# Cross-attention and feed-forward block on one core: two layer-norm scalings to ScalarE, residual add and shifts to GpSimd, bias by matmul

## The chip, the cores and the metric

One core of a Trainium2 chip. The metric is the device time of one execution in microseconds (us); lower is better.

## The reference, cut to what matters

```python
x = x + xattn0(layernorm(x), ctx, ctx)   # 16 batches x 8 heads; a head takes 16 rows of 256
x = x + ffn0(layernorm(x))               # 16 experts, one shared weight
x = x + xattn1(layernorm(x), ctx, mask)
x = x + ffn1(layernorm(x))               # half of the tokens, w1, gelu, w2

def layernorm(x): return (x - mean(x)) / sqrt(var(x) + 1e-5)

# xattn0: qk = qh . kh * scale; ret = softmax(qk) . vh      (x, ctx: [16, 128, 256])
# ffn0:   logits = xf @ router_w + router_b; S = softmax(logits); G, idx = top_k(S.T, 128)
#         out = xf[idx] @ expert_w + expert_b; y[idx] += G * out
```

## The kernel before, in words

The program runs in three stages. The first (to about 250 us) is the first attention with the expert product behind it; the second (to about 295 us) finds each expert's threshold digit by digit; the third is the second attention and the last feed-forward. The change touches the first stage; in the third it only puts buffers elsewhere.

The first stage handles two batches in a unit, eight units (`NU`), of 16 steps j: a step is one head of one batch. Every engine has its own list of instructions written by hand, `unit(...)` of each block, and `if j == ...` places extra work behind a step. Units 2 and 3 are one loop of the program, the others are written out. i is 0 for the unit's first batch and 1 for its second; the second is finished in the next unit.

- **TensorE** computes in step j the scores of a head that lies 8 steps ahead (`scores`, L1094), for the row maxima, and the transposed scores of the head 2 steps ahead (`scores_t`, L1107), for exp. Each has two banks, so scores wait until VectorE has reduced the bank, and transposed scores until ScalarE has taken theirs. Behind every fourth step comes the product with the values (`values`, L1121). `xn_t` transposes the normalised rows (L1144), `yw` multiplies them with the expert and router weights (L1150), `ctx_t` (L1137) and `max_t` (L1130) are transposes too.
- **VectorE** reduces row maxima (L531), makes the low part of the negated maxima (`neg_low`, L536), and finishes a batch: `gather_parts` (L542, L544) sorts numerators and denominators of even and odd heads, `invert` (L549), `bring_over` (L553, L556), `add_x1` (residual add L563, statistics L565 and L567), `scale_rows` (layer norm, L573), `take_yw` (L580, L581, both with a bias). For a later unit it computes the statistics of x (`stats_q`, L479 to L482) and the scaled queries (`scale_q`, L487).
- **ScalarE** does the exps (L895), `take_even` (L936, L937), `neg_high` (L901), the two DMA issues of `send_neg_max` (L906), `take_xnt` (L943), and the roundings of k and q to bf16: `high_k` (L918), `mid_k` (L922), `high_q` (L926), `mid_q` (L930).
- **GpSimd** does the remainders of these roundings (`rest_k` L336, `low_k` L341, `rest_q` L345, `low_q` L350), the inverse roots (L355, L357), `keep_rows` (L366) and `fill_values` (L374).
- **SyncE** writes the three parts of k and q to DRAM, stages the next unit's x and context (`load_stage`) and loads the stacks from DRAM.

Queries and keys are prepared three units ahead: unit u makes those of unit u + 3. All staging for unit u + 4 waits until q of unit u + 3 is split (`q_split`), since `ctx_stage` and `x_stage` exist once:

```python
sp.wait_ge(s["q_split"], u)                       # load_stage
dve.wait_ge(s["staged"], 32 * (u + 1))            # stats_q
```

## Time and profile before

| | us |
|---|---|
| median of 3 executions | 420.0 |
| lowest, highest | 419.33, 426.34 |
| the profiled execution, its own time | 422.43 |
| its span in the trace | 420.2 |
| VectorE busy | 317.7 (76%) |
| TensorE matmuls busy | 279.6 (67%) |
| ScalarE busy | 167.6 (40%) |
| GpSimd busy | 94.8 (23%) |

The span runs from the first to the last instruction; 2.2 us of the execution's own time lie outside it. PE is TensorE's matmuls, DVE VectorE, ACT ScalarE, POOL GpSimd, SPq and ACTq the instructions by which SyncE and ScalarE issue DMAs. In a row, `out<-in` are tiles by the program's names (digits are left out of some), then shapes and count. Instructions that follow one another closely overlap by up to 0.1 us in the trace, so a duration is a little more than the distance between two starts.

### The profile page before, as it was taken

To read this page: it belongs to the slowest core of one execution; us is meant where nothing else is said; L and a number is where in the kernel's file an instruction comes from. 1 tells how busy PE (TensorE), PEld (TensorE's weight loads), DVE (VectorE), ACT (ScalarE), POOL (GpSimd) and SP (SyncE) were. 2 spreads that over 40 slices of the span, in tenths; PEclk is the share of its full clock that TensorE was granted. 3 is DMA by queue.
4 is the path that set the end of the run, shared out by engine and by line. 5 is a ranking of instruction groups with operands and counts; after the bars stand their busy time and mean duration, and the time that the engine had idled before them with its cause. 6 is when DMAs were issued, how large, how long until landed. Compare 5 with 4: busy or idle time off the path is not lost.

```text
span 420.2 us, 7370 instructions
## 1 busy us (share of the span) xinstructions
PE 279.6 (67%) x1872; PEld 182.5 (43%) x1872; DVE 317.7 (76%) x989; ACT 167.6 (40%) x397; POOL 94.8 (23%) x222
## 2 busy tenths in 40 slices
PE   1134777777886877877778621001559999999996
PEld 0011333353442544444334310000438988888884
DVE  5847458899989889799986748888377888787631
ACT  4110543464654536464556500000111566445631
POOL 1101323352415224111111110000133322333200
PEclk9999975789698886899989965555555999999999
DMA  2789388959294581740000380000000000000001
GB/s 88 202 189 153 98 221 187 166 150 165 71 197 79 145 126 54 146 80 1 2 1 2 100 301 0 1 0 2 1 0 0 2 25 25 25 0 25 26 27 51
DMA packets 24379, 32.90 MB, mean 78 GB/s; under 512 B 4066, under 2 KB 22434, under 8 KB 22818
## 3 DMA queue, kind: packets, MB, share of 16 engines
q1 hardware_dynamic: 23842, 32.48, 33.5%
q10 hardware_dynamic: 512, 0.13, 0.2%
q8 instruction: 10, 0.16, 0.2%
q14 instruction: 15, 0.12, 0.1%
HBM read 24.02 MB, written 8.39 MB: 77 GB/s over the span
## 4 chain that ended last, share of the span: by engine, by line
DVE 35%; PE 33%; issue 12%; DMA 8%; ACT 4%; POOL 3%; SPq 2%; DVEq 1%; ACTq 1%; POOLq 0%
DVE row_max L531 7%; PE t_bank L1355 5%; PE pv_bank L1273 5%; PE pv_bank L1121 4%; DMA q_stack<-q_parts_dram 4%; DVE denom_inv L549 3%; PE score_bank L1094 3%; PE scoret_bank L1107 3%; PE t_bank L1150 2%; PE score_bank L1336 2%; DMA q_parts_dram<-q_parts 2%; ACT probs L895 2%; DMA q_stack<-neg_max 2%; PE score_bank L1303 2%; DVE junk L705 1%
## 5 line engine op out<-in xcount | busy, mean ns | idle before, releaser
L895 ACT ACTIVATE probs<-scoret_bank 128x512 f32<-128x512 f32 x128 | 73.1, 596 | 52.5 <-PE scoret_bank L1107 42.3
L531 DVE TENSOR_REDUCE row_max<-score_bank 128x2 f32<-128x512 f32 x112 | 74.4, 679 | 24.3 <-PE score_bank L1094 23.1
L1107 PE MATMUL scoret_bank<-q_stack,k_stack 98*128 98x256 bf16 (+1 forms) x256 | 54.6, 301 | 28.1 <-ACT probs L895 18.7
L1094 PE MATMUL score_bank<-k_stack,q_stack 96*128 96x256 bf16 (+1 forms) x240 | 53.6, 314 | 19.1 <-DMA q_stack<-q_parts_dram 11.0
L355 POOL TENSOR_SCALAR var_eps<-mv 128x1 f32<-128x1 f32 x48 | 9.2, 192 | 189.5 <-DVE mv L567 106.9
L1107 PEld LDWEIGHTS scoret_bank<-q_stack,k_stack 98*128 98x128 bf16 (+1 forms) x256 | 24.2, 104 | 46.6 <-ACT probs L895 20.5
L1121 PE MATMUL pv_bank<-probs,values_ones 128*32 128x256 f32 x512 | 42.0, 455 | 1.0 <-ACT probs L895 1.0
L1094 PEld LDWEIGHTS score_bank<-k_stack,q_stack 96*128 96x128 bf16 (+1 forms) x240 | 21.7, 105 | 47.8 <-issue 15.3
L1273 PE MATMUL pv_bank<-q_stack,k_stack 128*128 (+1 forms) x256 | 36.0, 285 | 0.4 <-ACT q_stack L1070 0.4
L1045 ACT COPY xnt<-score_bank 128x256 f32<-128x256 f32 x16 | 6.0, 373 | 74.6 <-PE score_bank L1294 74.6
L1273 PEld LDWEIGHTS pv_bank<-q_stack,k_stack 128*128 128x128 f32 x256 | 33.9, 202 | 1.3 <-issue 0.9
L1355 PE MATMUL t_bank<-k_stack,probs 128*128 128x256 f32 x128 | 29.4, 382 | 0.0
L357 POOL TENSOR_TENSOR rstd<-var_eps,minus_half 128x1 f32<-128x1 f32 x48 | 26.1, 543 | 8.8 <-POOL var_eps L355 8.8
L549 DVE RECIPROCAL denom_inv<-denom 128x256 f32<-128x256 f32 x16 | 27.7, 1732 | 0.0
L1355 PEld LDWEIGHTS t_bank<-k_stack,probs 128*128 128x128 f32 x128 | 23.7, 190 | 2.9
L1254 PE MATMUL t_bank<-count,same_expert 128*128 128x3 bf16 x15 | 2.8, 187 | 31.4 <-DVE equal L705 31.4
L1150 PE MATMUL t_bank<-wr_moving,xnt 128*128 128x272 f32 x64 | 22.0, 474 | 1.2 <-ACT xnt L943 1.2
L1064 ACT ACTIVATE probs<-pv_bank,b1s 128x128 f32<-128x128 f32 x64 | 17.6, 379 | 11.8 <-PE pv_bank L1273 11.7
L1121 PEld LDWEIGHTS pv_bank<-probs,values_ones 128*32 128x32 f32 x512 | 15.0, 122 | 16.2 <-issue 9.0
L1144 PE MATMUL t_bank<-ident,xn 128*128 128x128 f32 x32 | 7.0, 303 | 18.5 <-DVE xn L573 10.2
L1137 PE MATMUL t_bank<-ident,ctx_stage 128*128 128x128 f32 x32 | 7.6, 383 | 16.3 <-DMA x_stage<-in_x_dram 16.3
L1150 PEld LDWEIGHTS t_bank<-wr_moving,xnt 128*128 128x128 f32 x64 | 13.4, 234 | 8.1 <-issue 4.1
(182 smaller groups left out, 534.5 us busy)
## 6 DMA issues: line engine op xcount, KB each, us to landing
q_stack<-q_parts_dram SPq DMA_DIRECT2D x48, 128.0 KB, 6.9
k_parts_dram<-k_parts SPq DMA_DIRECT2D x24, 128.0 KB
q_parts_dram<-q_parts SPq DMA_DIRECT2D x24, 128.0 KB
k_stack<-k_parts_dram SPq DMA_DIRECT2D x8, 384.0 KB, 4.6
ctx_stage<-in_ctx_dram SPq DMA_DIRECT2D x8, 256.0 KB, 3.2
x_stage<-in_x_dram SPq DMA_DIRECT2D x8, 256.0 KB, 3.9
k_stack<-k_parts_dram SPq DMA_DIRECT2D x8, 256.0 KB, 5.3
xs<-in_x_dram SPq DMA_DIRECT2D x8, 256.0 KB, 7.3
```

The lines of the kernel that those rows point to most:

```text
L355: pool.tensor_scalar(work, variance, EPS, factor, ALU.add, ALU.mult).then_inc(s[summed], 1)
L357: pool.tensor_tensor(dst, work, minus_half[:, 0:dst.shape[1]], ALU.pow).then_inc(s[ready], 1)
L531: dve.tensor_reduce(row_max[:, i, :, h], score_bank[bank_of][:, :].rearrange("p (m n) -> p m n", m=2), AX.X, ALU.max).then_inc(s["max_done ...
L549: dve.reciprocal(denom_inv[:, i, :], denom[:, i, :]).then_inc(s["div_step"], 1)
L895: act.activation(probs[:, j % PROBS, :], scoret_bank[j % 2][:, :], ACT.Exp).then_inc(s["exp_done"], 1)
L1064: act.activation(hid[:, h, :], hid_bank[h // 4][:, (h % 4) * P:(h % 4 + 1) * P], ACT.Gelu_apprx_tanh, bias=b1s[:, h:h + 1]).then_inc(s["f_ ...
L1094: ins = pe.matmul(to[:, m * D:(m + 1) * D], q_stack[0:QROWS, slot, h, b_in, m * P:(m + 1) * P], k_stack[0:QROWS, slot, h, b_in, :], start= ...
L1107: ins = pe.matmul(scoret_bank[j % 2][:, k * D:(k + 1) * D], k_stack[0:SROWS, slot, h, b_in, k * P:(k + 1) * P], q_stack[0:SROWS, slot, h, ...
L1121: ins = pe.matmul(pv_bank[i][pair * Q:(pair + 1) * Q, odd * D:(odd + 1) * D], values_ones[:, i, k, pair, odd, :], probs[:, (j - GROUP + 1 ...
L1150: ins = pe.matmul(t1_bank[:, 0:D + NE], xnt[:, i, k, :], wr_moving[:, k, :], start=(k == 0), stop=(k == 1))
L1273: ins = pe.matmul(hid_bank[h // 4][:, (h % 4) * P:(h % 4 + 1) * P], w1s[:, k, h * P:(h + 1) * P], zg[:, k, bass.ds(P * t, P)], start=(k == ...
L1355: ins = pe.matmul(y_bank[:, 0:D], hid[:, h, :], w2s[:, h, :], start=(h == 0), stop=(h == NF - 1))
```

## The change

- `scale_q` and `scale_rows` leave VectorE and become ScalarE activations, scale * x + shift. The shift, minus mean times root, is computed by two further GpSimd instructions (`minus_shift`) behind each inverse root.
- The residual add of `add_x1` moves to GpSimd; VectorE keeps the statistics (`stats_x1`).
- `gather_parts` is one VectorE instruction over 512 columns instead of two over 256; ScalarE's two products stay two.
- The biases are added by TensorE: GpSimd splits them once into three bf16 parts (`split_bias`), and a third matmul in `yw` adds them. `take_yw` is then one copy of 272 columns, on ScalarE.
- Order: see the diff. `xn_t` stands at steps 2 and 10 (was 0 and 8); `stats_x1` at 6 and 14 (was in 5 and 13); `stats_q` of unit u + 4 at 13 (was 15); GpSimd's `low_q` behind the root of the unit's second batch.
- Eight buffers of the third stage come to lie in `k_stack`.

```diff
             def root_q(u):
                 inverse_root(rstd_q[:, :], mv0[:, :, 1], var16[:, :], float(C), "stats_q", "var_q", "root_q", u)
+                minus_shift(shift_q[:, :], mv0[:, :, 0], rstd_q[:, :], mean_rstd[:, 0:2], "root_q", "mean_q", "shift_q", u)
...
+            def minus_shift(dst, mean, root, work, ready, product, done, n):
+                wait_apart(pool, s[ready], n + 1)
+                pool.tensor_tensor(work, mean, root, ALU.mult).then_inc(s[product], 1)
+                wait_apart(pool, s[product], n + 1)
+                pool.tensor_tensor(dst, work, minus_one[:, 0:dst.shape[1]], ALU.mult).then_inc(s[done], 1)
...
+            def add_x1(b, u, i, first):
+                wait_apart(pool, s["div_step"], 4 * b + 4)
...
+                pool.tensor_tensor(x_new[:, i, :], gathered[:, i, 1, :], xs[:, b, :], ALU.add).then_inc(s["x1_done"], 1)
...
+            def split_bias():
...
+                pool.wait_ge(s["w_small"], 16 * 9)
+                step(pool.tensor_copy(bias_terms[:, 0, :], bias_f[:, :]))
...
                 fill_values(2 * u + 1, u, 1, first)
-                if parts and not first:
-                    low_q(u + 3)
                 if not first:
+                    add_x1(2 * u - 1, u - 1, 1, second)
                     root_rows(2 * u - 1, 1)
+                    if parts:
+                        low_q(u + 3)
                     keep_rows(x_new, 2 * u - 1, 1)
...
+                if first:
+                    split_bias()
+                add_x1(2 * u, u, 0, first)
                 root_rows(2 * u, 0)
                 keep_rows(x_new, 2 * u, 0)
...
-            def scale_q(u):
-                dve.wait_ge(s["root_q"], u + 1)
-                for i in range(2):
-                    ins = dve.tensor_scalar(qn[:, i, :], x_stage[:, i, :], mv0[:, i, 0:1], rstd_q[:, i:i + 1],
-                                            ALU.subtract, ALU.mult)
-                ins.then_inc(s["q_ready"], 1)
...
-                dve.scalar_tensor_tensor(denom[:, i, :], odd_heads, low[:, 0:1], sum_high[:, i, :],
+                dve.scalar_tensor_tensor(gathered[:, i].rearrange("p k n -> p (k n)"), pv_bank[i][:, :], high[:, 0:1],
+                                         low_part[:, i].rearrange("p k n -> p (k n)"),
                                          ALU.mult, ALU.add).then_inc(s["div_step"], 1)
-                dve.scalar_tensor_tensor(numer[:, i, :], odd_heads, high[:, 0:1], num_low[:, i, :],
-                                         ALU.mult, ALU.add).then_inc(s["div_step"], 1)
...
-                    if j == 13:
-                        add_x1(b, u, 0, first)
-                    if j == 14 and not first:
-                        take_yw(a)
-                    if j == 15:
-                        scale_rows(b, 0, first)
-                    if j == 15 and more_parts and not first:
+                    if j == 14:
+                        stats_x1(b, 0)
+                    if j == 13 and more_parts and not first:
                         stats_q(u + 4)
...
+            def take_yw(b):
+                act.wait_ge(s["yw_ready"], b + 1)
+                act.copy(y_ext[:, b, :], t1_bank[:, 0:D + NE]).then_inc(s["yw_done"], 1)
+
+            def scale_q(u):
+                act.wait_ge(s["shift_q"], u + 1)
+                for i in range(2):
+                    ins = act.activation(qn[:, i, :], x_stage[:, i, :], ACT.Identity, bias=shift_q[:, i:i + 1],
+                                         scale=rstd_q[:, i:i + 1])
+                ins.then_inc(s["q_ready"], 1)
...
-                ins.then_inc(s["yw_ready"], 1)
...
+                ins = pe.matmul(t1_bank[:, 0:D + NE], ones_bf[0:3, 0:P], bias_parts[:, :], start=False, stop=True)
```

ScalarE now has `scale_rows` behind `take_even` (steps 1 and 9), `scale_q(u + 3)` at step 1 (4 in unit 1), `take_yw` at 7 and 14, and `high_q`, `mid_q`, `take_xnt` one or two steps later than before.

The first place is VectorE in the loop of units 2 and 3, from the scaling of the gathered numerators (L556, now L603) of a unit's first batch to the end of the unit. Before:

```order
L556 TENSOR_TENSOR numer<-numer,denom_own 128x256
...
L531 TENSOR_REDUCE row_max<-score_bank 128x2
...
L563 TENSOR_TENSOR x_new<-numer,xs 128x256
L565 BN_STATS st<-x_new 128x6
L567 BN_AGGR mv<-st 128x2
...
L573 TENSOR_SCALAR xn<-x_new,mv,rstd 128x256
...
L479 BN_STATS st<-x_stage 128x6 x2
```

and after:

```order
L603 TENSOR_TENSOR gathered<-gathered,denom_own 128x256
...
L578 TENSOR_REDUCE row_max<-score_bank 128x2
L531 REGISTER_ALU
L532 ISA
L534 BN_STATS st<-x_stage 128x6 x2
...
L537 BN_AGGR mv<-st 128x2
L577 REGISTER_ALU
L578 TENSOR_REDUCE row_max<-score_bank 128x2
L608 BN_STATS st<-x_new 128x6
L610 BN_AGGR mv<-st 128x2
```

The residual add, the scaling and the expert rows are gone, and the statistics of the staged x (for the queries of a later unit) and one more row maximum now stand ahead of those of x_new.

The second place is GpSimd in the same loop, from the filling of the values to the copy of x_new, with `q_parts` the low part of q that ends `q_split`. Before:

```order
L374 COPY values_ones<-vt 128x8x16
L350 TENSOR_TENSOR q_parts<-q_rest,q_parts 128x512
L355 TENSOR_SCALAR var_eps<-mv 128x1
L357 TENSOR_TENSOR rstd<-var_eps,minus_half 128x1
L366 ISA
L366 COPY xs<-x_new 128x256
```

and after:

```order
L423 COPY values_ones<-vt 128x8x16
...
L391 TENSOR_TENSOR x_new<-gathered,xs 128x256
L366 TENSOR_SCALAR var_eps<-mv 128x1
L368 TENSOR_TENSOR rstd<-var_eps,minus_half 128x1
L372 TENSOR_TENSOR mean_rstd<-mv,rstd 128x1
L374 TENSOR_TENSOR shift_x<-mean_rstd,minus_one 128x1
L361 TENSOR_TENSOR q_parts<-q_rest,q_parts 128x512
L394 COPY xs<-x_new 128x256
```

`q_parts` moved from ahead of the second batch's root to behind it, the residual add and the two products of the shift.

## Rows read from the trace of the kernel before

**Rows 1.** Busy us by engine in stretches between negated maxima; PEclk is the granted clock
```profile
94.19:107.89 13.70, 9.28 (x72) 4.70 (x72) 13.25 (x28) 6.76 (x15) 4.22 (x7) 0.92 0.79 138
107.89:119.90 12.01, 10.11 (x76) 5.87 (x76) 10.40 (x22) 7.19 (x16) 4.45 (x9) 0.81 0.44 123
196.75:207.28 10.53, 8.04 (x72) 4.57 (x72) 10.10 (x23) 5.82 (x13) 1.68 (x5) 1.00 0.00 1
```

**Rows 2.** Groups by line, 60 to 225 us: busy us, mean ns of one, idle before
```profile
L573 DVE TENSOR_SCALAR xn<-x_new,mv,rstd 128x256 f32<-128x256 f32 x13 | 7.7, 596 | 1.0 <-POOL rstd L357 0.8
L936 ACT ACTIVATE sum_high<-pv_bank,high 128x256 f32<-128x256 f32 x14 | 6.6, 472 | 3.8 <-PE pv_bank L1121 3.7
L487 DVE TENSOR_SCALAR qn<-x_stage,mv,rstd_q 128x256 f32<-128x256 f32 x10 | 6.4, 676 | 0.0
L563 DVE TENSOR_TENSOR x_new<-numer,xs 128x256 f32<-128x256 f32 x13 | 6.2, 479 | 0.0
L544 DVE SCALAR_TENSOR_TENSOR numer<-pv_bank,high,num_low 128x256 f32<-128x256 f32 x13 | 6.0, 463 | 0.0
L580 DVE TENSOR_TENSOR y<-t_bank,eb_rows 128x256 f32<-128x256 f32 (+1 forms) x12 | 5.0, 413 | 0.0
L581 DVE TENSOR_TENSOR logits<-t_bank,eb_rows 128x16 f32<-128x16 f32 (+1 forms) x12 | 2.0, 164 | 0.0
```

**Rows 3.** Waits between 97 and 160 us, ScalarE: us in total, times, longest us
```profile
ACT k_parts L922 <- POOL k_rest L336: 10.7, 3, 3.8
```

**Rows 4.** Timeline of VectorE: start us, us, instruction
```profile
124.29 0.43 DVE L556 TENSOR_TENSOR numer<-numer,denom_own 128x256 f32<-128x256 f32 x1
...
126.26 0.18 DVE L567 BATCH_NORM_AGGREGATE mv<-st 128x2 f32<-128x6 f32 x1 [0.15 <-DVE st L565]
...
127.98 1.18 DVE L573 TENSOR_SCALAR xn<-x_new,mv,rstd 128x256 f32<-128x256 f32 x1
129.08 0.74 DVE L479 BATCH_NORM_STATS2 st<-x_stage 128x6 f32<-128x256 f32 x2
...
130.51 1.29 DVE L531 TENSOR_REDUCE row_max<-score_bank 128x2 f32<-128x512 f32 x2 [0.29 <-issue]
131.71 1.36 DVE L487 TENSOR_SCALAR qn<-x_stage,mv,rstd_q 128x256 f32<-128x256 f32 x2
...
133.60 0.40 DVE L536 SCALAR_TENSOR_TENSOR neg_max<-t_bank,neg_max 8x256 bf16<-8x256 f32 x1
...
140.76 0.18 DVE L567 BATCH_NORM_AGGREGATE mv<-st 128x2 f32<-128x6 f32 x1
...
193.31 0.41 DVE L573 TENSOR_SCALAR xn<-x_new,mv,rstd 128x256 f32<-128x256 f32 x1
```

**Rows 5.** Timeline of GpSimd: start us, us, instruction
```profile
6.43 0.72 POOL L357 TENSOR_TENSOR rstd_q<-var,minus_half 128x2 f32<-128x2 f32 x1 [0.18 <-POOL var L355]
...
126.64 0.19 POOL L355 TENSOR_SCALAR var_eps<-mv 128x1 f32<-128x1 f32 x1 [9.63 <-DVE mv L567]
127.01 0.54 POOL L357 TENSOR_TENSOR rstd<-var_eps,minus_half 128x1 f32<-128x1 f32 x1 [0.18 <-POOL var_eps L355]
...
127.86 1.15 POOL L336 TENSOR_TENSOR k_rest<-ctx_stage,k_parts 128x512 f32<-128x512 f32 x1
...
137.10 1.16 POOL L350 TENSOR_TENSOR q_parts<-q_rest,q_parts 128x512 bf16<-128x512 f32 x1 [1.57 <-ACT q_parts L930]
```

**Rows 6.** Timeline of ScalarE: start us, us, instruction
```profile
123.02 0.62 ACT L918 CAST k_parts<-ctx_stage 128x512 bf16<-128x512 f32 x1
...
129.04 0.62 ACT L922 CAST k_parts<-k_rest 128x512 bf16<-128x512 f32 x1 [3.43 <-POOL k_rest L336]
```

**Rows 7.** Timeline of SyncE's issues: start us, us, instruction
```profile
138.29 2.03 SPq L242 DMA_DIRECT2D q_parts_dram<-q_parts  x3
...
141.09 0.42 SPq L228 DMA_DIRECT2D x_stage<-in_x_dram  x1
```

**Rows 8.** DMA issues of the page: count, KB each, us from issue to landing
```profile
x_stage<-in_x_dram SPq DMA_DIRECT2D x8, 256.0 KB, 3.9
```

More of the change, by code:

```diff
@@ L365, in keep_rows, with step @@
+            def add_x1(b, u, i, first):
+                wait_apart(pool, s["div_step"], 4 * b + 4)
+                wait_apart(pool, s["x_loaded"], 16 * (u + 1))
+                if not first:
+                    wait_apart(pool, s["xn_ready"], b - 1)
+                    wait_apart(pool, s["kept"], b - 1)
+                pool.tensor_tensor(x_new[:, i, :], gathered[:, i, 1, :], xs[:, b, :], ALU.add).then_inc(s["x1_done"], 1)
             def keep_rows(rows, b, i):
                 pool.tensor_copy(xs[:, b, :], rows[:, i, :]).then_inc(s["kept"], 1)
+            def split_bias():
+                n = [0]
+                def step(ins):
+                    n[0] += 1
+                    ins.then_inc(s["bias_step"], 1)
+                    pool.wait_ge(s["bias_step"], n[0])
+                pool.wait_ge(s["w_small"], 16 * 9)
+                step(pool.tensor_copy(bias_terms[:, 0, :], bias_f[:, :]))
+                step(pool.tensor_tensor(bias_left[:, 0, :], bias_f[:, :], bias_terms[:, 0, :], ALU.subtract))
+                step(pool.tensor_copy(bias_terms[:, 1, :], bias_left[:, 0, :]))
+                step(pool.tensor_tensor(bias_left[:, 1, :], bias_left[:, 0, :], bias_terms[:, 1, :], ALU.subtract))
+                step(pool.tensor_copy(bias_terms[:, 2, :], bias_left[:, 1, :]))
+                for part in range(3):
+                    wait_apart(pool, s["ident_done"], 1)
+                    ins = pool.tensor_scalar(bias_kept[:, part, :], bias_terms[:, part, :], ident[0:3, part:part + 1], None, ALU.mult)
+                step(ins)
+                step(pool.tensor_tensor(bias_sum[:, :], bias_kept[:, 0, :], bias_kept[:, 1, :], ALU.add))
+                pool.tensor_tensor(bias_parts[:, :], bias_sum[:, :], bias_kept[:, 2, :], ALU.add).then_inc(s["bias_done"], 1)
@@ L567, in add_x1 @@
                 dve.bn_aggr(mv[:, i, :], st3[:, i, :]).then_inc(s["stats1"], 1)
-            def scale_rows(b, i, first):
-                if not first:
-                    dve.wait_ge(s["xn_t"], b - 1)
-                dve.wait_ge(s["root1"], b + 1)
-                dve.tensor_scalar(xn[:, i, :], x_new[:, i, :], mv[:, i, 0:1], rstd[:, i:i + 1],
-                                  ALU.subtract, ALU.mult).then_inc(s["xn_ready"], 1)
-            def take_yw(b):
-                dve.wait_ge(s["yw_ready"], b + 1)
-                if is_n(b, 0):
-                    dve.wait_ge(s["w_small"], 16 * 9)
-                dve.tensor_tensor(y[:, b, :], t1_bank[:, 0:D], eb_rows[:, 0:D], ALU.add)
-                dve.tensor_tensor(logits[:, b, :], t1_bank[:, D:D + NE], eb_rows[:, D:D + NE], ALU.add).then_inc(s["yw_done"], 1)
             def next_maximum(u, n):
@@ L609, in unit @@
                         stats_q(u + 3)
-                    if j == (3 if second else 1) and not first and parts:
-                        scale_q(u + 3)
                     if j == 2 and scored and not first:
@@ L619, in unit @@
                         bring_over(a, 1)
-                    if j == 5 and not first:
-                        add_x1(a, u - 1, 1, second)
-                    if j == 7 and not first:
-                        scale_rows(a, 1, second)
-                    if j == 8 and not first:
-                        take_yw(2 * u - 2)
+                    if j == 6 and not first:
+                        stats_x1(a, 1)
                     if j == 10 and scored and not first:
@@ L912, in take_vt, with scale_rows @@
                          t0_bank[:, :]).then_inc(s["vt_done"], 1)
+            def take_yw(b):
[7 more added lines that the diff above has]
+                ins.then_inc(s["q_ready"], 1)
+            def scale_rows(b, i, second):
+                if not second:
+                    act.wait_ge(s["xn_t"], b - 1)
+                act.wait_ge(s["shift_x"], b + 1)
+                act.activation(xn[:, i, :], x_new[:, i, :], ACT.Identity, bias=shift_x[:, i:i + 1],
+                               scale=rstd[:, i:i + 1]).then_inc(s["xn_ready"], 1)
             def high_k(u):
@@ L1217, in unit @@
                         values(STEPS * u + j, 2 * u + j // NH, j, first)
-                    if j == 0 and not first:
+                    if j == 2 and not first:
                         if not second:
@@ L1223, in unit @@
                         if second:
-                            pe.wait_ge(s["w_small"], 16 * 9)
+                            pe.wait_ge(s["bias_done"], 1)
                         yw(2 * u - 2, 0)
-                    if j == 8 and not first:
+                    if j == 10 and not first:
                         pe.wait_ge(s["yw_done"], 2 * u - 1)
                         xn_t(2 * u - 1, 1)
-                    if j == 11 and not first:
+                    if j == 12 and not first:
                         yw(2 * u - 1, 1)
```

127 lines of the change are left out of this document (74 added, 53 removed).

## The prediction

> **What bounds the kernel now.** I read the busy time by stretch first, cut at VectorE's negated maxima (neg_max, L536): there is one behind step 2 and one behind step 10 of every unit, so a stretch is half a unit. A half that begins at step 2 I call the first, one that begins at step 10 the second [rows 1]. In the second half from 94.19 VectorE is busy 13.25 of 13.70 us, in one without work for a later unit (196.75) 10.10 of 10.53; TensorE has 9.3 and 8.0, ScalarE 6.8 and 5.8. So VectorE is the fullest engine nearly everywhere, and moving work off it looks right. The first half from 107.89 is different: VectorE 10.40 of 12.01, TensorE 10.11, at a granted clock of 0.81, which means that TensorE spent part of it at 1.2 instead of 2.4 GHz. There VectorE is not alone.
>
> Then the waits. ScalarE stands still 10.7 us in three waits for GpSimd's k_rest [rows 3], one at the start of each of units 2, 3 and 4: ScalarE's `mid_k` waits for k_rest, and GpSimd gets to k_rest only behind the root of x_new's statistics. One case in order of time: the numerators are scaled at 124.29, the statistics (mv) are aggregated at 126.26, GpSimd takes them at 126.64, k_rest starts at 127.86, ScalarE's k_parts at 129.04 [rows 4 to 6]. ScalarE's next exps are queued behind it, and TensorE's next scores behind those. Before the change this costs little, because VectorE is busy all the while: xn takes 1.18 us there, the statistics of x_stage follow, and qn takes 1.36 [rows 4]. The wait lies beside VectorE's work; the question is what happens when that work goes.
>
> **What leaves VectorE.** By means per batch [rows 2]: xn 0.60, x_new 0.48, y and logits 0.41 + 0.16, one of the two gathers (0.46, of which the wider instruction takes back an estimated 0.27, 256 more columns, so 0.2); per unit two qn of 0.68. Over 16 batches: 9.5 + 7.7 + 9.2 + 3 and 10.8 for the 16 qn, together some 40 us of busy time; less than that on the path, since starts stand up to 0.1 us closer than durations. The wider gather is in no row: between 0.46 (nothing for the width) and 0.93 (twice the instruction), I take 0.73.
>
> Part of this was waiting for the port. xn takes 0.41 us at 193.31, with GpSimd idle, and 1.18 at 127.98, where k_rest runs beside it [rows 4, 5]. The Trainium skill (SBUF — State Buffer, section on the two separate sides) says that VectorE and GpSimd share a port pair under an exclusive lock, and that a VectorE operation in a two-port mode, or one with two SBUF inputs against a GpSimd operation that reads SBUF, can be shut out for the other's whole duration. The two xn rows agree. By that rule the change is worth more than its instruction counts at 1.0 us per slow xn or qn, but the scaling of the numerators, with two SBUF inputs, stays on VectorE beside a GpSimd with more to do.
>
> **What comes instead.** ScalarE gets per batch one scaling and one copy of 272 columns, per unit two scalings of q. No row has them; the nearest is sum_high, 0.47 us [rows 2]. Between 0.3 and 0.6 each I take 0.37 on the path. GpSimd gets the residual add and two products behind every root. k_rest, 512 columns, takes 1.15 [rows 5], so I take 0.6 for the add (bounds 0.4, its copy-like floor, and 1.15). A product of one column lies between the 0.19 of var_eps and the 0.54 of the power; spaced as var_eps to rstd (126.64 to 127.01) two are 0.75, at the power's price 1.4. I take 0.75.
>
> **Units 1 to 3, second half.** Here the order has moved. Before, mv follows the numerators' scaling by 1.97 (124.29 to 126.26). Now the residual add of 0.45 is gone from between, but the statistics of x_stage (0.74 and two aggregations, 1.1 together) and one more row maximum (0.60, from two in 130.51 to 131.71) stand ahead: + 1.25. GpSimd adds 0.75 ahead of k_rest. So ScalarE's k_parts comes 4.75 + 2.0 = 6.75 us behind the numerators, and nothing of what VectorE lost helps. From k_parts (129.04) to neg_max (133.60) were 4.56, ending in qn. Now ScalarE must do k_parts 0.5, an exp 0.5, two products 0.7, three scalings 1.1, an exp 0.5 and the high part 0.3 before VectorE's neg_max: 3.65, 0.9 less. With 0.15 from the gather this half becomes 0.95 us longer.
>
> **First half.** 1.4 us leave VectorE (x_new, xn, y and logits, gather). TensorE was busy 10.11 of 12.01 and slow for part of it [rows 1], just after the pause that the ScalarE wait makes; the pause grows. I take 1.2 of the 1.4.
>
> **The stage load.** q_parts starts 8.06 us after k_parts (137.10 after 129.04). SyncE then writes it (138.29) and issues x_stage at 141.09; landing takes 3.9 [rows 5 to 8]: 7.9 from q_parts to landed, so 16.0 behind k_parts, and the first user, ScalarE's L918, came at 123.02, 6 us before the next k_parts. Now q_parts stands behind the second batch's statistics. These came 11.7 behind k_parts (140.76); now 0.9 + 0.5 + 0.1 earlier and one row maximum later, 10.8; root and shift add 1.25 + 0.75, so q_parts starts at 12.8 and x_stage lands at 20.7. VectorE wants it 5.8 before the next k_parts, at 19.9 in a unit of 25.7. So a new wait of some 0.8 us comes up in VectorE with the row maxima behind it, half of which I count as hidden. Units 1 to 3: 3 x (0.95 - 1.2 + 0.4) = + 0.5.
>
> **Unit 4 on.** No statistics or k_rest for a later unit follow. Unit 4 gives 1.2 + 1.4. The halves at 185, 196 and 207 run at full clock with VectorE 96% busy [rows 1]: 1.3, 1.2 and 0.9 (row maxima end in the last). Together - 6.0. In unit 7 VectorE has no maxima and ScalarE leads: two more instructions a batch, but `xn_t` no longer stalls TensorE at step 0: + 0.2. The end of the stage is a bare chain: shift 0.75, add on GpSimd 0.3, third matmul 0.2, gather less 0.15: + 1.1.
>
> **Start.** q of units 0 and 1 is on the path to the first stack: qn follows the root of 6.43 at once; the shift adds 0.75 in each, of which the second overlaps with DMAs in part: + 1.2. `split_bias` is 11 GpSimd instructions of 272 columns, queued in unit 0 ahead of the first residual add, for which VectorE waits. At 0.19 + 0.18 each they are 4 us, at half of k_rest's 1.15 plus 0.18 they are 8. I take 6.5, and cost it at nothing: TensorE has that time filled with scores and values at the low clock. Without that cover it is up to 3 us.
>
> The later stages do the same work. Sum: + 1.2 + 0.5 - 6.0 + 0.2 + 1.1 = - 3.0 us against the profiled execution's 422.43 (span 420.2 and 2.2 around it), so 419.4; against the median of the runs shown, 420.0, it is 417.0.
>
> **Rivals.**
> *VectorE's load is the time.* For it: 96% busy in [rows 1], and the port waits. Of the 40 us of busy time 16 would then show in the path of units 1 to 6 (2.6 a unit), less 2 at the ends: about 405. Against it: the three ScalarE waits hang on GpSimd, and TensorE's 10.1 of 12.0. 0.25.
> *The stage load takes over.* If TensorE's low clock or the products at the power's price delay the second batch's statistics by 2 us more, x_stage lands 2.5 to 3 us late in units 1 to 3; ScalarE's L918 and VectorE's statistics wait at step 13 and the whole loop runs at the pace of q_parts to staging to q_parts. 3 x 2.8 = + 8.4 on my sum, 425: slower than before. It decides from a landing later than 21.5 us behind k_parts. 0.14.
> *The bias split is uncovered* and the first unit stalls for its full length: + 3, 420. 0.04.
>
> **The numbers.** My forecast 0.57, 417, by itself 412 to 421. Faster by over 2% (below 411.6; 2% is about what a measurement of this kernel tells from no change) comes from the first rival and a small part of mine: 0.26. Slower by over 2% (above 428.4) only from the tail of the second: 0.05. The range of 8 in 10 reaches into both: 406.5 to 424.
>
> **What would show it.** Right: VectorE's busy time falls by 30 us or more and the first stage shortens by less than 5; ScalarE's wait for k_rest grows from 3.6 to about 5 us a case; the second half of units 1 to 3 is no shorter than 13.7; ScalarE's L918 waits for the DMA at step 13; halves from 185 on take about 1.2 less. Wrong: second halves of 12 us or less, or k_parts within 5 us of the scaled numerators; a granted clock near 1 in first halves would also move it down.

## The result and the profile after

The changed kernel took 429.8 us (median of 4 runs, 428.8 to 430.4); the kernel before, run beside it on the same chip, 423.2. Two of its four runs were slow ones (426.3), so the ratio takes the other two (419.3 and 420.0): 1.024 (1.020 to 1.027), slower, where 417.0 us and a range of 406.5 to 424 were forecast. The profiled execution's span went from 420.2 to 427.0 us, 6.8 more; that is less than the 9.8 between the medians 420.0 and 429.8, because the profiled execution of before (422.4 us) was longer than its median.

The first view is the page of the profile after: busy us by engine, and TensorE's granted clock in 40 slices.

```profile
PE 286.4 (67%) x1888; PEld 182.9 (43%) x1888; DVE 287.8 (67%) x894; ACT 188.6 (44%) x445; POOL 121.8 (29%) x296
...
PEclk9999985768698695999988965555555999999999
```

VectorE gave up the work (317.7 to 287.8 us), ScalarE and GpSimd took it (+ 21.0 and + 27.0), and the time still rose. The windows between negated maxima, the same cut as [rows 1], say where: the second half that began at 94.19, the first half behind it, the next second half, and the one that began at 196.75. A row has the start and end, the length, the busy us (and count) of PE, PEld, DVE, ACT and POOL, the granted clock, the DMA share and GB/s.

```profile
96.41:111.55 15.14, 9.70 (x72) 4.50 (x70) 10.05 (x22) 8.04 (x19) 5.76 (x12) 0.77 0.86 169
111.55:122.79 11.24, 10.14 (x79) 5.62 (x78) 9.31 (x16) 7.88 (x18) 4.96 (x11) 0.86 0.24 58
122.79:139.27 16.48, 10.31 (x74) 5.13 (x74) 10.15 (x21) 8.36 (x19) 6.20 (x14) 0.88 0.81 168
200.17:210.37 10.20, 8.16 (x76) 4.46 (x75) 8.92 (x16) 6.68 (x15) 2.66 (x8) 1.00 0.01 2
```

VectorE is busy 10.15 of 16.48 us in a stretch that took 13.70 before. No engine is full there: the time is waits. Three rows, between 97 and 160 us as in [rows 3] (us in total, times, longest):

```profile
DVE row_max L578 <- PE score_bank L1142: 11.9, 16, 2.6
...
ACT k_parts L949 <- DMA x_stage<-in_x_dram: 8.8, 3, 3.4
...
ACT k_parts L953 <- POOL k_rest L347: 6.6, 2, 3.4
```

The wait for the staged context and x is new; the one for k_rest fell from 10.7 us in three to 6.6 in two. One case of each in ScalarE's timeline (start us, us, instruction, idle before):

```profile
121.42 0.60 ACT L942 ACTIVATE xn<-x_new,shift_x,rstd 128x256 f32<-128x256 f32 x1 [0.47 <-POOL shift_x L374]
...
129.46 0.62 ACT L949 CAST k_parts<-ctx_stage 128x512 bf16<-128x512 f32 x1 [3.23 <-DMA x_stage<-in_x_dram]
...
135.20 0.62 ACT L953 CAST k_parts<-k_rest 128x512 bf16<-128x512 f32 x1 [3.26 <-POOL k_rest L347]
```

and GpSimd's list of the same stretch, in which the four small instructions of the root and shift stand ahead of q's low part, whose end releases SyncE's writes and then the stage load:

```profile
117.59 0.73 POOL L391 TENSOR_TENSOR x_new<-gathered,xs 128x256 f32<-128x256 f32 x1 [1.16 <-DVE gathered L603]
119.66 0.19 POOL L366 TENSOR_SCALAR var_eps<-mv 128x1 f32<-128x1 f32 x1 [1.34 <-DVE mv L610]
120.03 0.56 POOL L368 TENSOR_TENSOR rstd<-var_eps,minus_half 128x1 f32<-128x1 f32 x1 [0.18 <-POOL var_eps L366]
120.76 0.19 POOL L372 TENSOR_TENSOR mean_rstd<-mv,rstd 128x1 f32<-128x1 f32 x1 [0.18 <-POOL rstd L368]
121.13 0.19 POOL L374 TENSOR_TENSOR shift_x<-mean_rstd,minus_one 128x1 f32<-128x1 f32 x1 [0.18 <-POOL mean_rstd L372]
121.28 1.15 POOL L361 TENSOR_TENSOR q_parts<-q_rest,q_parts 128x512 bf16<-128x512 f32 x1
```

The span by stretch, from the starts of negated maxima and of the maximum over the router's logits, which ends the first stage, before and after (us), with the forecast's terms:

| stretch | before | after | moved | forecast |
|---|---|---|---|---|
| start, to unit 1's first maximum | 81.54 | 82.85 | + 1.3 | + 1.2 |
| units 1 to 3 | 79.75 | 85.60 | + 5.9 | + 0.5 |
| unit 4 and the halves up to 217.24 | 55.95 | 51.93 | - 4.0 | - 6.0 |
| last negated maximum to logits' maximum | 33.39 | 36.73 | + 3.3 | + 1.3 |
| behind it | 169.6 | 169.9 | + 0.3 | 0 |

### The profile page after: what moved, and what is told of

Its sections match the earlier page's. It is cut to its first block, busy times and chain, and to the rows that moved or that the text cites. A ratio compares the mean times of both kernels' runs of the same rounds, so it can differ in the third digit from the quotient of the medians.

```text
span 427.0 us, 7539 instructions
## 1 busy us (share of the span) xinstructions
PE 286.4 (67%) x1888; PEld 182.9 (43%) x1888; DVE 287.8 (67%) x894; ACT 188.6 (44%) x445; POOL 121.8 (29%) x296
## 4 chain that ended last, share of the span: by engine, by line
DVE 26%; PE 24%; issue 16%; POOL 11%; ACT 8%; DMA 8%; SPq 3%; ACTq 2%; DVEq 1%; POOLq 1%
DMA x_stage<-in_x_dram 4%; POOL rstd L368 3%; ACT probs L908 3%; PE pv_bank L1169 3%; DVE row_max L578 3%; PE scoret_bank L1155 3%; PE pv_bank L1322 3%; PE t_bank L1198 3%; PE t_bank L1404 2%; PE score_bank L1142 2%; PE score_bank L1385 2%; DVE denom_inv L596 2%; POOL var_eps L366 2%; DMA q_stack<-q_parts_dram 2%; SPq L253 2%
## 5 line engine op out<-in xcount | busy, mean ns | idle before, releaser
L1155 PE MATMUL scoret_bank<-q_stack,k_stack 98*128 98x256 bf16 (+1 forms) x256 | 57.6, 317 | 45.0 <-ACT probs L908 38.1
L1142 PE MATMUL score_bank<-k_stack,q_stack 96*128 96x256 bf16 (+1 forms) x240 | 55.9, 328 | 13.3 <-DMA q_stack<-q_parts_dram 12.1
L1169 PE MATMUL pv_bank<-probs,values_ones 128*32 128x256 f32 x512 | 43.8, 471 | 0.7 <-ACT probs L908 0.7
L1322 PEld LDWEIGHTS pv_bank<-q_stack,k_stack 128*128 128x128 f32 x256 | 33.5, 200 | 1.3 <-issue 0.9
L391 POOL TENSOR_TENSOR x_new<-gathered,xs 128x256 f32<-128x256 f32 x16 | 11.6, 726 | 59.2 <-DVE gathered L603 59.2
L596 DVE RECIPROCAL denom_inv<-gathered 128x256 f32<-128x256 f32 x16 | 27.8, 1738 | 0.1
L1169 PEld LDWEIGHTS pv_bank<-probs,values_ones 128*32 128x32 f32 x512 | 15.4, 125 | 17.0 <-issue 10.8
L1198 PE MATMUL t_bank<-wr_moving,xnt 128*128 128x272 f32 x64 | 20.3, 445 | 0.9 <-ACT xnt L974 0.9
L590 DVE SCALAR_TENSOR_TENSOR gathered<-pv_bank,high,low_part 128x512 f32<-128x512 f32 x16 | 11.7, 733 | 7.2 <-ACT low_part L968 7.2
```

The lines of the kernel that those rows point to most:

```text
L596: dve.reciprocal(denom_inv[:, i, :], gathered[:, i, 0, :]).then_inc(s["div_step"], 1)
L1142: ins = pe.matmul(to[:, m * D:(m + 1) * D], q_stack[0:QROWS, slot, h, b_in, m * P:(m + 1) * P], k_stack[0:QROWS, slot, h, b_in, :], start= ...
L1155: ins = pe.matmul(scoret_bank[j % 2][:, k * D:(k + 1) * D], k_stack[0:SROWS, slot, h, b_in, k * P:(k + 1) * P], q_stack[0:SROWS, slot, h, ...
L1169: ins = pe.matmul(pv_bank[i][pair * Q:(pair + 1) * Q, odd * D:(odd + 1) * D], values_ones[:, i, k, pair, odd, :], probs[:, (j - GROUP + 1 ...
L1198: pe.matmul(t1_bank[:, 0:D + NE], xnt[:, i, k, :], wr_moving[:, k, :], start=(k == 0), stop=False)
L1322: ins = pe.matmul(hid_bank[h // 4][:, (h % 4) * P:(h % 4 + 1) * P], w1s[:, k, h * P:(h + 1) * P], zg[:, k, bass.ds(P * t, P)], start=(k == ...
```

## The experiments

The medians below stand beside runs of the kernel before on the same chip, which was 420.1 to 420.8 us (for after see above); changes are given as ratios to it. To compare kernels by stretch I use four lengths, each from the profiled execution's trace: from the second negated maximum (48.5 us in after), early in unit 0, over units 1 to 3 to the first negated maximum of unit 4 ("loop"), the four halves behind unit 4's first ("halves", unit 4's first itself is in none), from the last negated maximum to the logits' maximum ("tail"), and the second negated maximum itself ("start").

Each length is of one execution, and that can lie 2.6 us below its kernel's median (e1: 425.0 against 427.6) or 2.4 above (before: 422.4 against 420.0). So loops that differ by less than some 3 us are not told apart. The halves repeat far better: e1, e3, e4, e9 and after have 40.1 to 40.3.

| kernel | us | ratio | start | loop | halves | tail |
|---|---|---|---|---|---|---|
| before | 420.1 to 420.8 | 1 | 48.0 | 113.3 | 43.5 | 33.4 |
| after | 429.8 | 1.024 | 48.5 | 120.0 | 40.3 | 36.7 |
| e1_lowq_early | 427.6 | 1.020 | 48.7 | 115.4 | 40.1 | 37.3 |
| e2_stats_late | 423.4 | 1.008 | 49.1 | 114.1 | 41.2 | 37.5 |
| e3_both_orders | 424.5 | 1.011 | 49.6 | 115.2 | 40.1 | 36.7 |
| e4_restk_before_root | 420.4 | 0.999 | 49.2 | 109.2 | 40.1 | 38.7 |
| b1_restk_early | 420.3 | 0.998 | 48.5 | 111.9 | 42.2 | 33.4 |
| e5_scalings_back | 416.0 | 0.987 | 48.4 | 111.9 | 37.9 | 33.5 |
| e6_scalings_alone | 417.2 | 0.991 | 50.3 | 112.5 | 39.6 | 33.2 |
| e7_back_and_orders | 413.2 | 0.980 | 48.9 | 109.4 | 37.9 | 33.5 |
| e8_q_only | 421.1 | 1.003 | 49.5 | 113.6 | 37.9 | 33.7 |
| e9_rows_only | 425.3 | 1.014 | 47.9 | 116.6 | 40.1 | 37.3 |
| e10_no_shift | 418.3 | 0.995 | 49.0 | 115.3 | 37.9 | 33.8 |
| e11_one_product | 425.6 | 1.013 | 49.3 | 117.9 | 39.1 | 34.7 |
| e12_one_product_orders | 414.8 | 0.986 | 49.8 | 106.0 | 39.1 | 37.1 |
| e13_q_only_orders | 412.8 | 0.980 | 48.9 | 108.3 | 37.9 | 33.7 |

**Orders.** The first question was which queue order makes the two waits of ScalarE. Three edits, alone and together, to the changed kernel:

```diff
# e1: q's low part ahead of the root (and shift) of the second batch
-                    root_rows(2 * u - 1, 1)
                     if parts:
                         low_q(u + 3)
+                    root_rows(2 * u - 1, 1)
# e2: statistics of q where they were before
-                    if j == 13 and more_parts and not first:
+                    if j == 15 and more_parts and not first:
                         stats_q(u + 4)
# e3: both. e4: both, and
+                if more_parts and not first:
+                    rest_k(u + 4)
                 root_rows(2 * u, 0)
...
-                    rest_k(u + 4)
```

> The changed kernel with one order edit: GpSimd's low part of q (q_parts) ahead of the root and shift of the second batch, behind the residual add. Theory A (the loop q split -> staging -> statistics is what made the change slow): x_stage is issued 3 to 4 us earlier in units 1 to 3, ScalarE's waits for the DMA (8.8 us in three) and VectorE's (2.1) are gone, and the time falls by 6 to 8 us from 429.8, to about 422 to 424. Theory B (the chain x_new add on GpSimd, statistics, root, two products, k_rest sets the pace by itself): the waits for the DMA go, but ScalarE waits for k_rest as much longer, and the time falls by less than 2 us.

> The changed kernel with one order edit: VectorE's statistics of the staged x for unit u + 4 back at step 15, behind those of x_new. Theory A (the staging loop alone): ScalarE still waits for the DMA; x_new's statistics no longer stand behind the landing, so k_rest comes up to 2.5 us earlier in three units: 3 to 7 us less, 423 to 427. Theory B (the chain to k_rest): this edit takes 1.7 us out of that chain in three units, 5 us less, and more than the other order edit gives. A result within 1 us of the changed kernel speaks against both.

> Both order edits together. Theory A: little more than the first alone (422), since the landing no longer holds anything. Theory B: about what the second gives alone. If both links are in series, the savings add: 9 to 11 us, 419 to 421.

> Both order edits, and GpSimd's k_rest for unit u + 4 ahead of the root of x_new's statistics (it needs only ScalarE's rounding of the context). ScalarE's three waits for k_rest (3.3 us each) should go. If ScalarE's standing still is what keeps VectorE idle in the second halves, 7 to 10 us less than with the two order edits alone: 410 to 414, below the kernel before. If TensorE at the low clock is the limit, less than 3 us.

Each order did to its own wait what was expected of it, but the times fell by less than hoped. e1's median is only 2.2 us below after's, which their intervals don't separate (theory B); e2's is 6.3 below; e4's is 4.1 below e3's, between the 7 to 10 and the "less than 3" that I had written. With q's low part early, ScalarE's waits between 84 and 190 us read:

```profile
ACT k_parts L953 <- POOL k_rest L347: 15.0, 3, 5.0
...
ACT k_parts L949 <- DMA x_stage<-in_x_dram: 0.4, 1, 0.4
```

The stage load is no longer waited for (8.8 to 0.4), and k_rest is waited for the longer (9.8 to 15.0). With the statistics late it is the other way round:

```profile
ACT k_parts L949 <- DMA x_stage<-in_x_dram: 11.2, 3, 4.3
...
ACT k_parts L953 <- POOL k_rest L347: 2.0, 2, 1.1
```

Each alone takes some 5 us out of the loop (4.6 and 5.8), both together no more (4.8): it looks as if the waits hand the time to one another, though of such sums one profile each can't tell 1 us. Only with k_rest ahead of the root as well do both go (2.1 and 1.0 us in all), and the loop is 10.8 us shorter than after's. Of that the tail gave 2.0 back, and the start and unit 4's first half 1.6. TensorE's granted clock rose along with it: in the second halves of units 2 and 3 it was 0.88 and 0.72 in after, 0.86 and 0.87 in e3, 1.00 and 0.98 in e4. What of the 10.8 us is shorter waiting and what is the faster clock, the runs don't separate.

The last of these edits was also made alone to the kernel before:

> The kernel before with one order edit: GpSimd's k_rest for unit u + 4 ahead of the root of x_new's statistics. ScalarE's three waits of 3.6 us go. If they lie beside VectorE's work, as the prediction said, the time stays within 1 us of 420. If they hold the kernel before too, it falls by 4 to 8 us.

Its profiled execution is shorter by 1.3 us in the loop and by 1.4 in the halves (there by the clock, see below), but over ten runs the ratio is 0.998 (0.995 to 1.001), which can't be told from none. So the orders cure what the change brought; they were no gain that lay ready.

**The two halves of the change apart.** e5 is the changed kernel with both scalings on VectorE again, with mean and root (the rows' one step later than before), and no shift; e6 is the kernel before with the two scalings on ScalarE, the shift on GpSimd and the places of transposes and roundings that go with them; e7 is e5 with the three order edits.

```diff
# e5, in VectorE's unit; the same instructions leave ScalarE's
+                    if j == 0 and not first:
+                        scale_rows(2 * u - 2, 0, second)
+                    if j == (3 if second else 1) and not first and parts:
+                        scale_q(u + 3)
+                    if j == 8 and not first:
+                        scale_rows(a, 1, second)
```

> The changed kernel with both scalings back on VectorE and no shift on GpSimd; sums, biases and all orders as changed. If order and residual add carry the loss, most of it stays: the loop through staging is only 0.75 us a unit shorter, ScalarE still waits for the DMA: 425 to 428. If the scalings carry it (0.5 us each on ScalarE, 0.75 of shift in three chains, the bare last unit), the time falls to 421 or below.

> The kernel before with the two scalings alone moved to ScalarE, the shift on GpSimd, and the positions of transposes that go with them; q_parts, residual add and statistics where they were. If order and residual add carry the loss: VectorE gains 2.5 us a unit and ScalarE's wait for k_rest grows by 0.75 in three units, 416 to 420. If the scalings carry it: 424 to 428.

> Scalings back on VectorE with the three order edits (q_parts early, statistics late, k_rest early). Against the run of the three order edits with the scalings on ScalarE (420.4): the last unit, where ScalarE leads and VectorE idles, gets back 3 to 5 us, the full-clock halves lose 0.5 each: 414 to 418. If the scalings on ScalarE were worth their place there, 421 or more.

This was the surprise of the study: the sums, biases and order alone are faster (0.987, 0.982 to 0.992), the scalings alone are faster (0.991, 0.988 to 0.995), and together they are slower (1.024). e7 too was off, a little better than its 414 to 418: I had VectorE's scalings cost 0.5 us a half there, and the halves are 0.6 each shorter than e4's.

The four halves show why moving VectorE's work pays only once. In before VectorE is the fullest engine in them (38.8 us busy of 43.5). The first of the four ran at a granted clock of 0.86 there:

```profile
173.71:185.56 11.85, 9.75 (x73) 5.28 (x72) 10.23 (x22) 5.77 (x13) 1.68 (x5) 0.86 0.79 141
```

In b1, which has the same instructions in it, it ran at 1.00 and took 10.53 us, 1.3 less; so at full clock before is to be taken at b1's 42.2 us. From this e5 takes 4.3 out, e6 2.6 and after, which has both, only 1.8. The first window is e5's, the second after's, four halves each:

```profile
171.66:209.54 37.88, 31.47 (x283) 16.98 (x283) 35.11 (x67) 23.77 (x52) 9.31 (x24) 1.00 0.34 68
```

```profile
180.05:220.38 40.33, 32.24 (x289) 17.46 (x289) 33.84 (x62) 26.71 (x57) 11.10 (x34) 1.00 0.33 64
```

The second has less work on VectorE and 2.45 us more time, at a granted clock of 1.00 in both. Something other than an engine's load sets its pace.

**Which scaling, and which part of it.** e8 puts only the rows' scaling back to VectorE, e9 only q's; e10 leaves both on ScalarE and takes GpSimd's products away. It leaves minus mean times root out of the computation and adds the mean itself, so it is no layer norm, but every other instruction stands.

```diff
# e10, the rows' scaling; q's likewise, and minus_shift is gone behind both roots
-                act.wait_ge(s["shift_x"], b + 1)
-                act.activation(xn[:, i, :], x_new[:, i, :], ACT.Identity, bias=shift_x[:, i:i + 1],
+                act.wait_ge(s["root1"], b + 1)
+                act.activation(xn[:, i, :], x_new[:, i, :], ACT.Identity, bias=mv[:, i, 0:1],
                                scale=rstd[:, i:i + 1]).then_inc(s["xn_ready"], 1)
```

> After, with the scaling of the stage's rows (xn) back on VectorE in one operation with mean and rstd; the scaling of q stays on ScalarE with its GpSimd product. After is 429.8 us and both scalings back 416.0 us (x_stage's transfer 5.4 us of ScalarE's wait in place of 8.8). Theory A (the pair shift plus scaling sits on the chain softmax, x_new, q in every unit, where q's product stands ahead of the write that the stage load follows, so q carries the interaction): most of the loss stays, 425 to 430 us, second halves of the looped units still 15 us or more, VectorE's waits for x_stage near 2 us. Theory B (the rows' scaling carries it: on ScalarE it stands behind k_parts and waits for a product that GpSimd only makes behind its sums, so root rows come late to TensorE): 416 to 420 us, second halves near 14. If each carries its half: 421 to 424 us.

> After, with the scaling of q back on VectorE in one operation and the rows' scaling left on ScalarE with its GpSimd product: the mirror of the run before. Theory A (q carries the interaction): 416 to 420 us, q_parts again within 13 us behind k_parts and ScalarE's wait for x_stage down to 5 us or less. Theory B (the rows carry it): 425 to 430 us. Each its half: 421 to 424 us. If the losses of the two runs add up to less than 13.8 us, the two scalings hurt only together.

> After, without GpSimd's two shift products: ScalarE takes the mean itself as bias, so the subtraction of mean times rstd is left out of the computation; every other instruction stands as in after. In the trace of after one product costs about 0.75 us from rstd to its end with the write of the copy, ScalarE's scaling 0.50 us to the next instruction. Theory A (the wait through GpSimd is the loss, because it lies ahead of q_parts and of the rows in every unit): 16 units by one to two products is 12 to 20 us at most, and the time falls to 417 to 420 us. Theory B (the loss is that ScalarE, which takes its instructions in order, now carries both scalings amid probs and the parts, and GpSimd's product is a small piece of it): 425 to 429 us.

The products are most of the loss: without them the same kernel takes 418.3 us, 11.5 less, of the 13.8 that both scalings cost (by the ratios 12 of 15.4). That q's scaling carries it (theory A of e8 and e9) fell: q's back gains 4.5, the rows' back 8.7. They add up to 13.2 (by the ratios 12.7 of 15.4), and each ratio is good to 1.4 to 3 us either way, so an interaction between the two scalings isn't seen, and a small one couldn't be. The halves and the tail divide the kernels built from after cleanly: where the rows' scaling waits for two products they take 40.1 to 40.3 (41.2 in e2, whose first half ran at a clock of 0.85) and 36.7 to 38.7 us, where it waits for none 37.9 and 33.5 to 33.8, on whichever engine it runs. (e6, built from before, stands apart. Its halves take 39.6, and VectorE is busy 36.9 of them. Its tail takes 33.2 though it has both products: for the tail the products alone are not the cause, see below.) The waits of ScalarE between 175 and 215 us, a little less than the four halves, have one row in after that e10 lacks:

```profile
ACT xn L942 <- POOL shift_x L374: 2.5, 4, 0.8
```

2.5 us, against 2.5 us by which the halves differ. One case in after, in ScalarE's timeline:

```profile
197.56 0.47 ACT L968 ACTIVATE low_part<-pv_bank,low 128x256 f32<-128x256 f32 x1
198.79 0.60 ACT L942 ACTIVATE xn<-x_new,shift_x,rstd 128x256 f32<-128x256 f32 x1 [0.77 <-POOL shift_x L374]
199.30 0.58 ACT L908 ACTIVATE probs<-scoret_bank 128x512 f32<-128x512 f32 x1
199.78 0.36 ACT L914 ACTIVATE neg_max<-t_bank 8x256 bf16<-8x256 f32 x1
```

and without the products:

```profile
192.41 0.47 ACT L965 ACTIVATE low_part<-pv_bank,low 128x256 f32<-128x256 f32 x1
192.90 0.60 ACT L939 ACTIVATE xn<-x_new,mv,rstd 128x256 f32<-128x256 f32 x1
193.41 0.58 ACT L905 ACTIVATE probs<-scoret_bank 128x512 f32<-128x512 f32 x1
193.88 0.36 ACT L911 ACTIVATE neg_max<-t_bank 8x256 bf16<-8x256 f32 x1
```

Both timelines have the instructions in the program's order, the exp 0.51 us behind xn. Behind xn stand that exp, the negated maxima, whose end VectorE waits for, and further exps, for which TensorE's next transposed scores wait. A wait of 0.45 to 0.77 us for the shift moves all of them once in every half: (40.33 - 37.86) / 4 = 0.62 us a half. So in the halves it isn't the engine that the scaling went to, but the two links that the move put ahead of it.

**Length or presence.** e11 makes the shift in one GpSimd operation, e12 does so in e4.

```diff
-                pool.tensor_tensor(work, mean, root, ALU.mult).then_inc(s[product], 1)
-                wait_apart(pool, s[product], n + 1)
-                pool.tensor_tensor(dst, work, minus_one[:, 0:dst.shape[1]], ALU.mult).then_inc(s[done], 1)
+                for c in range(dst.shape[1]):
+                    ins = pool.tensor_scalar(dst[:, c:c + 1], mean[:, c:c + 1], root[:, c:c + 1], -1.0, ALU.mult, ALU.mult)
+                ins.then_inc(s[done], 1)
```

> After, with the shift made by one GpSimd operation (mean times rstd times -1 with the rstd as a per-partition operand, two of them without a wait in between for q) in place of two products with a wait between. The wait goes and with it about 0.37 us of the 0.75 (for q some 0.2). Without any product the time was 418.3, with two 429.8 us. Theory A (the time follows the length of the chain through GpSimd): 423 to 426 us, second halves of the looped units half way between the two. Theory C (it is a step: what costs is that there is any instruction of GpSimd between the root and ScalarE's scaling, with its own wait behind sums and low parts): 428 to 430 us. Theory D (only the last 0.37 us pushes an order over): 418 to 420 us.

> The same one operation for the shift, in the kernel with all three order edits (low_q ahead of the root, statistics of q late, rest_k ahead of root rows), which was 420.4 us with two products and 413.2 us with the scalings back on VectorE. Theory A: half of the products' cost goes here too, 415 to 418 us. Theory B (the order edits had already covered the products, and the rest of the distance to 413.2 us is ScalarE's own work and the clock in the last unit): 419 to 421 us.

GpSimd's timeline of e12 has the shorter chain:

```profile
103.18 0.57 POOL L368 TENSOR_TENSOR rstd<-var_eps,minus_half 128x1 f32<-128x1 f32 x1 [0.18 <-POOL var_eps L366]
103.96 0.27 POOL L373 TENSOR_SCALAR shift_x<-mv,rstd 128x1 f32<-128x1 f32 x1 [0.21 <-POOL rstd L368]
```

From the root's end (103.75) to the shift's (104.23) it is 0.48 us, against 0.73 with two products (120.59 to 121.32). The halves follow: 37.9, 39.1 and 40.3 us for none, one and two, and the times too: 418.3, 425.6 and 429.8. It is a length, not a step. In the loop, with the orders mended, the scalings on ScalarE seem even to pay: 106.0 us in e12 against 109.4 in e7, which has them on VectorE. What e12 wins there it gives back in the halves (1.2 us) and the tail (3.6).

e13 puts the pieces together: q on ScalarE with one operation, rows on VectorE without any, the three orders.

> The sum of the pieces that were seen to pay: q scaled on ScalarE with its shift in one GpSimd operation, the rows scaled on VectorE without any product, and the three order edits. If the stretches add as the traces of the other runs have them (49.5 us to the second negated maximum; 106 us for the looped part as with one product and orders, or 109.4 as with both scalings on VectorE and orders; 11.5 for the half behind it; 37.9 for the four halves at full clock; 33.6 from the last negated maximum to the logits' maximum; 169.8 behind it and 2.2 around the span), the time is 410.5 to 414 us against 413.2 with both scalings on VectorE and 414.8 with both on ScalarE. Theory A (what costs is a GpSimd product ahead of the rows' scaling, not ScalarE's scaling itself): 409 to 413 us. Theory B (a mixed form is worse, as q_only was, 421.1 against 416.0, because q's product holds q back): 414 to 418 us.

412.8 us (0.980, 0.975 to 0.986) is within what its stretches promised, and faster than before and after; from e7's 413.2 it can't be told. These two are the best found. The loop came to 108.3 us, not the 106.0 of e12; whether the rows' scaling on ScalarE is worth that in the loop, one profile each doesn't show.

## Why the prediction was wrong

**Of the signs**, three held: VectorE's busy time fell by 30 us, the second halves of units 1 to 3 did not get shorter, ScalarE's `high_k` (L918 before, L949 now) waits for the DMA. Two failed. The wait for k_rest did not grow to 5 us a case; it was 3.3 (9.8 in three between 84 and 190 us), since the wait for the DMA came first, and grew to 5.0 only in e1, which takes that away. The halves from 185 on became 0.5 us shorter each, not 1.2. The start moved by 1.3 us (1.2 forecast), but by luck, since not where I had it: of 1.3 us at the first negated maximum 0.3 was left at the third, and the rest of unit 0 brought 1.0 more.

**"What comes instead" mis-sized the scaling on ScalarE.** I took 0.37 us from between 0.3 and 0.6, near sum_high's 0.47 [rows 2]; the trace of after has, between 60 and 225 us,

```profile
L391 POOL TENSOR_TENSOR x_new<-gathered,xs 128x256 f32<-128x256 f32 x13 | 9.4, 725 | 47.0 <-DVE gathered L603 47.0
L942 ACT ACTIVATE xn<-x_new,shift_x,rstd 128x256 f32<-128x256 f32 x12 | 7.2, 602 | 4.9 <-POOL shift_x L374 4.9
```

so 0.60 us, and 0.51 from its start to the next (198.79 to 199.30 above). The Trainium skill (ScalarE: Activation LUTs, section on what a table load costs) gives an activation 186 ns and 0.833 ns a column, about 93 ns for each per-partition operand, and an overlap of some 93 ns between neighbours; an estimate from these figures is 0.59 and 0.49 us here. The trace agrees, with 0.60 and 0.51, and the page would have been the better source than my nearest row. The add took 0.73 where I took 0.6; the gather (0.73) and the pair of products (0.73 for 0.75) were right. These sizes are small: e10, which has the scaling and the add at full price, is faster than before.

**"Unit 4 on" is the first step that failed.** It gave - 6.0; measured - 4.0. The shift's 0.75 us was charged to second halves of units 1 to 3, to the start and to the end, and not to the other halves. There I let VectorE's relief count in full, as if the rows' scaling could wait for GpSimd beside it. It is 2.5 us in four halves (e10 or e5 against after), and its mechanism is the waiting xn with exps and negated maxima behind it, which I never named: I had not asked what is queued behind the new wait on ScalarE. The relief itself was there: in e10, without the products, this stretch is 49.0 us, 7.0 shorter than before's. My ground for it was in part misread, though. "VectorE 96% busy" holds for the half at 196.75 alone; at 185.56 it was 91% and at 207.28 84%. And 1.3 us of all these gains are the clock of 0.86 that before had in the half at 173.71 and the others did not.

**The tail** has the same chain, and grew by 3.3 us where 1.3 were forecast (0.2 for unit 7, 1.1 for the end). Without products it is 33.8. Of the 2.9 us more in after the last shift in the bare chain is 0.75 by its length; most of the rest goes with TensorE's clock. From the last negated maximum to the logits' maximum the windows of e10, e11, e12, after and e4 read:

```profile
213.30:247.10 33.80, 22.10 (x171) 10.78 (x169) 16.30 (x29) 19.17 (x41) 7.72 (x18) 0.85 0.37 125
```

```profile
217.76:252.42 34.66, 21.19 (x171) 10.46 (x169) 16.30 (x29) 19.34 (x41) 8.71 (x22) 0.87 0.36 122
```

```profile
205.76:242.84 37.08, 25.55 (x171) 12.34 (x169) 16.29 (x30) 19.30 (x41) 8.75 (x22) 0.75 0.34 114
```

```profile
220.38:257.11 36.73, 24.17 (x171) 11.79 (x169) 16.29 (x29) 19.42 (x41) 9.21 (x26) 0.78 0.34 115
```

```profile
210.99:249.70 38.71, 26.96 (x171) 12.40 (x169) 16.30 (x29) 19.35 (x41) 9.22 (x26) 0.69 0.32 109
```

The same 171 matmuls take 22.1 us at a mean granted clock of 0.85 and 27.0 at 0.69. e11 and e12 have the same instructions there, with one product, and lie 2.4 us apart; after and e4, with two, 2.0. In the first 23 us of the tail the granted clock is 1.00 in e10 and e11, 0.85 in e12 and after, 0.70 in e4. So at the full clock one product costs the tail 0.9 us (e10 to e11), and what two would cost without the slower clock no run shows. My sum for the tail had no term for the clock.

**"Units 1 to 3" is the larger failure**: + 0.5 forecast, + 5.9 measured. The second halves grew by 1.4, 2.8 and 1.5 us where I had 0.95 each; the first halves moved by + 0.9, - 0.8 and - 0.05 where I had - 1.2 each. The prediction's "First half" took 1.4 us off VectorE and believed nearly all of it, though the stretch showed TensorE with 10.1 of 12.0 busy at a clock of 0.81; that TensorE work is still 10.1 us in after (second window above). "The stage load" had the mechanism and nearly the place: q_parts starts 13.8 us behind k_parts (121.28 after 107.48) where I had 12.8, x_stage lands 22.0 behind it where I had 20.7 and the deciding point at 21.5. So had the chain to k_rest: k_parts comes 6.8 us behind the scaled numerators (107.48 after 100.66) where I had 6.75, and 8.1 where the statistics had waited for the stage load (135.20 after 127.06). So rival 2, to which I gave 0.14, is what the loop does in after, and its 425 us was my nearest number. But it isn't the whole: e1 takes that wait away and stays at 427.6, because k_rest is then the late one.

What neither the forecast nor a rival had, and what e1, e2 and e4 speak for without proving it, is that two closed chains of nearly equal length run through the loop, one over k_rest and one over q_parts and the stage load, and the two products lie in both (before k_rest and, with the new order, before q_parts). Easing one leaves the other; I had priced them one after the other and let the gain of the first halves pay for both.

**Rival 1**, VectorE's load, falls: it was nearly the time in the halves of before, and stopped being it as soon as 3 to 4 us had left. **Rival 3**, the bias split, didn't happen at its price. Its ten instructions took 7.5 us (69.49 to 77.00; 6.5 for eleven forecast) and held up the first residual add (at 76.96, with its input ready at 73.4), but the stretch around it (62.84 to 81.54 before, 63.12 to 82.85 after) grew by 1.0 us, not by 3.

## What to carry to other kernels

When work leaves the fullest engine, list for each new wait what stands behind it on its own in-order engine; here a 0.73 us link cost 0.62 us in every half, although the engine that the work came from had been relieved. Two changes that each relieve the same engine need not add: here, once another chain was as long, the second brought mainly its side costs. Keep a short helper (a shift, a sign) out of the chain, or in one instruction, before moving the large operation that needs it.

## What the runs showed of the hardware

- A dependent GpSimd operation on one column costs 0.37 us: 0.19 and a gap of 0.18. The one with a per-partition operand takes 0.27 and a gap of 0.21, so folding two into one saved 0.25, not 0.37.
- TensorE's granted clock differs between kernels that have the same instructions in a stretch, and so does its length. e4 had 0.69 in its tail against after's 0.78, and took 2.0 us more; e12 had 0.75 against e11's 0.87, and took 2.4 more. A gain made ahead can be lost in part that way, but it isn't the early arrival as such: e1, e2, e3 and e9 came into the tail 4.4 to 5.0 us earlier than after, with the same 0.78. What decides between the two levels there was not tried and stays open.
- That the order edits are worth 10.8 us in the loop with two products, 12.0 with one and 2.5 with the scalings on VectorE is in keeping with the two chains above. But no run shortened one chain by a known amount alone, and the clock in the loop moved along, so the split is argued and not shown.
